# A decoder layer on one core: context values made after the attention, the prologue's loads and steps reordered, the last tile's steps moved

## The reference

```
x = x + attention(layernorm(x))
x = x + cross(layernorm(x), context)
x = x + ffn(layernorm(x))
```

```
K, V = context @ Wh (per head, 2 heads of 128)
A    = max(|sum over batches (Q K^T / sqrt(128) * decay)|, 1)
out  = (relu(x @ wg) * groupnorm(A V)) @ wo
```

## Time and profile before

| what | value |
| --- | --- |
| device time, three runs | 262.43 us median (260.69 to 265.61) |
| profiled execution | 264.52 us |
| its span | 262.4 us |
| PE, DVE, ACT, POOL busy | 239.2, 148.8, 129.0, 92.3 us |
| prologue, to the masks of tile 0 | 0 to 23.7 us |
| tiles 0 to 6 | 23.7 to 102.0 us |
| last tile, to cross_mix | 102.0 to 125.8 us |
| cross attention, router, experts, output | 125.8 to 262.4 us |

### The profile page before, as it was taken

How to read it: one execution, slowest core, us unless ns; L and a number is a source line. 1 busy time by engine, 2 the same in 40 slices (tenths; PEclk the granted TensorE clock), 3 DMA queues, 4 the chain that set the end, 5 groups by cost and what they waited for, 6 DMA issues and landing times.

```text
span 262.4 us, 5169 instructions
## 1 busy us (share of the span) xinstructions
PE 239.2 (91%) x1628; PEld 176.7 (67%) x1628; DVE 148.8 (57%) x451; ACT 129.0 (49%) x465; POOL 92.3 (35%) x109
## 2 busy tenths in 40 slices
PE   8768879899999999968787999989999999999995
PEld 6437356666675677847565878756777777777783
DVE  1456827798788877532789569845233232232275
ACT  1124787898898978830052522503433443333340
POOL 2110201111211111010266101464777777777461
PEclk9959999999999999988999999999999999999999
DMA  7999987500000620000001300032232333334396
GB/s 209 238 344 346 368 202 189 152 5 4 4 0 2 224 91 0 4 0 2 0 0 40 122 0 1 5 100 80 71 111 100 102 100 100 106 102 112 104 317 227
DMA packets 20852, 28.10 MB, mean 107 GB/s; under 512 B 2833, under 2 KB 17819, under 8 KB 20827
## 3 DMA queue, kind: packets, MB, share of 16 engines
q1 hardware_dynamic: 16683, 19.01, 24.1%
q0 software_dynamic: 2976, 8.13, 10.2%
q10 hardware_dynamic: 1167, 0.65, 1.0%
HBM read 21.62 MB, written 6.16 MB: 106 GB/s over the span
## 4 chain that ended last, share of the span: by engine, by line
PE 54%; issue 13%; ACT 11%; DMA 9%; DVE 8%; POOL 2%; SPq 1%; ACTq 1%; POOLq 0%; DVEq 0%
PE bank L882 13%; PE bank L894 8%; ACT pr_s L991 7%; PE bank L813 7%; PE bank L522 5%; DMA lnkv_s<-in_ln_kv 4%; PE bank L863 3%; DMA x_s<-expert_out 2%; PE bank L873 2%; PE bank L527 2%; PE bank L570 2%; PE bank L555 2%; PE bank L645 1%; PE bank L498 1%; ACT prT L981 1%
## 5 line engine op out<-in xcount | busy, mean ns | idle before, releaser
L991 ACT ACTIVATE pr_s<-bank,mx 128x128 f32<-128x128 f32 x128 | 45.3, 383 | 9.6 <-DVE mx L1221 9.0
L882 PE MATMUL bank<-gu_s,bxT 128*128 x124 | 41.7, 460 | 0.2 <-DVE bxT L1544 0.2
L1550 DVE TENSOR_TENSOR pr_s<-bank,pr_s 128x176 f32<-128x176 f32 x31 | 10.6, 341 | 51.7 <-ACT pr_s L1150 50.9
L483 POOL DMA_INDIRECT expert_out<-by,prT x31 | 31.1, 1004 | 15.1 <-ACT by L981 7.7
L478 POOL DMA_INDIRECT qx_s<-ffn_in,prT x31 | 30.1, 972 | 14.5 <-issue 8.2
L981 ACT ACTIVATE prT<-bank 128x512 f32<-128x512 f32 (+1 forms) x63 | 30.7, 497 | 2.2 <-PE bank L570 1.2
L894 PE MATMUL bank<-dn_s,prT 88*128 x124 | 31.7, 379 | 0.0
L991 ACT ACTIVATION_READ_ACCUMULATOR pr_s<-bank,mx 128x1 f32 x128 | 28.6, 223 | 0.0
L882 PEld LDWEIGHTS bank<-gu_s,bxT 128*128 128x128 f32 x124 | 21.2, 190 | 7.2 <-issue 0.4
L570 PE MATMUL bank<-tab,pr_s 128*128 128x128 f32 x128 | 19.5, 275 | 5.4 <-ACT prT L981 2.8
L1221 DVE TENSOR_REDUCE mx<-bank 128x4 f32<-128x512 f32 x32 | 20.4, 682 | 5.9 <-PE bank L555 5.8
(11 more groups left out here) (192 smaller groups left out, 428.8 us busy)
## 6 DMA issues: line engine op xcount, KB each, us to landing
gu_s<-in_w_gu SPq DMA_DIRECT2D x8, 704.0 KB, 8.7
dn_s<-in_w_dn SPq DMA_DIRECT2D x4, 704.0 KB
qx_s<-in_ctx_in SPq DMA_DIRECT2D x2, 512.0 KB, 10.5
ffn_in<-x_s SPq DMA_DIRECT2D x4, 256.0 KB, 2.1
cv_s<-expert_out SPq DMA_DIRECT2D x4, 256.0 KB, 4.3
x_s<-expert_out SPq DMA_DIRECT2D x4, 256.0 KB, 6.0
out<-x_s SPq DMA_DIRECT2D x7, 128.0 KB, 4.0
gu_s<-in_x_t SPq DMA_DIRECT2D x1, 768.0 KB, 12.4
```

Of the source, the lines that this page charges most:

```text
L483: pool.indirect_dma_start(expert_out[:], bass.IndirectOffsetOnAxis(ap=idx[:, 1, k:k + 1], axis=0), by[:, k % RB, :], None).then_inc(dma_sc ...
L882: last = mm(bank[2 + i % 2][:, 0:2 * I], bxT[:, i % 2, k, :], gu_s[:, k, bass.ds(e, 1), :], start=k == 0, stop=k == KD - 1)
L991: last = nc.scalar.activation(pr_s[:, n % 2, h, :], score_bank(n)[:, h * T:(h + 1) * T], ACT.Exp, bias=mx[:, n % 4, h:h + 1], accum_out=de ...
L1550: V.tensor_tensor(bh[:, i % 2, :], bank[2 + i % 2][:, I:2 * I], bs[:, i % 2, :], ALU.mult).then_inc(dve_hidden, 1)
```

## The change

- **Loads.** The layer-norm constants become columns of the table, and identity, rope, head and layer-norm columns come in one DMA on ACT's queue, which then has three DMAs where it had six. x tile 1 moves from sixth to third place on SP's queue. The context is held in the first half of gu_s[:, 1], where it can stay longer; the two expert-weight loads for that half move behind a wait for all context values, ahead of the ffn_in stores on SP's queue.
- **Prologue order.** `qk_transpose(0)` directly follows `keys_values(0)` and stands ahead of `latent_transpose(1)`; on VectorE `q_out(0)` goes ahead of `latent_normalize(1)`; the statistics of x tiles 4 to 7 move into tile 0.
- **Context keys and values.** Both context-key steps of group 1 stay in tile 0 but stand later; all four context-value steps move behind the attention, with their copies.
- **Last tile.** Gates (2,1) move behind `out_project(6)`, the cross scores are spread between the last steps, the denominators of tile 7 are computed ahead of the variance of tile 6, the last denominators' transpose goes to bank 5 and the last probabilities' to bank 0, and `out_project(7)` stands ahead of `cross_transpose(6)`.

The core of the diff:

```diff
-        lnq_s = sb("lnq_s", [128, 2])
-        lnkv_s = sb("lnkv_s", [KPH, 2, 2])
+        lnq_s = tab[:, C_LN:C_LN + 2]
+        lnkv_s = tab[0:KPH, C_LN + 2:C_LN + 6].rearrange("p (k n) -> p k n", k=2)
...
-        cT = qx_s[:].rearrange("p b k t -> p (b k t)")[:, 0:B * D].rearrange("p (h b t) -> p h b t", h=XH, b=B)
+        cT = gu_s[:, 1, 0:E // 2, :].rearrange("p e n -> p (e n)")[:, 0:B * D].rearrange("p (h b t) -> p h b t", h=XH, b=B)
...
             sp.dma_start(x_s[:, 0:1, :], xv[:, 0:1, :]).then_inc(ld_x[0], 16)
+            sp.dma_start(x_s[:, 1:2, :], xv[:, 1:2, :]).then_inc(ld_x[1], 16)
             sp.dma_start(wht_s, wh_t.rearrange("h p n -> p h n")).then_inc(ld_wh_t, 16)
             sp.dma_start(cT[:, :, 0:4, :], ctx_in[:, :, 0:4, :]).then_inc(ld_ctx0, 16)
             sp.dma_start(wkv_s[:], w_kv.rearrange("(k p) n -> p k n", p=KPH)).then_inc(ld_w_kv, 16)
-            sp.dma_start(x_s[:, 1:2, :], xv[:, 1:2, :]).then_inc(ld_x[1], 16)
...
-            for k, e in ((0, 0), (0, 4), (0, 8), (0, 12), (1, 0), (1, 4)):
+            for k, e in ((0, 0), (0, 4), (0, 8), (0, 12)):
                 expert_weights(k, e)
...
+            sp.wait_ge(pe_ctx_values, B // 2)
+            expert_weights(1, 0)
+            expert_weights(1, 4)
...
             def ctx_values(g, j):
                 if g == 0:
                     pe.wait_ge(ld_wh, 16)
-                    pe.wait_ge(act_ctx_keys, j + 1)
+                    pe.wait_ge(act_probs_T, NC * B - 2) if j else pe.wait_ge(act_exp, NC * B - 1)
                 else:
-                    pe.wait_ge(act_keys_values, 3) if j else pe.wait_ge(dve_qk_T, 2)
+                    pe.wait_ge(act_ctx_values, j + 1)
...
             queries(0)
             keys_values(0)
+            qk_transpose(0)
             latent_transpose(1)
-            ctx_values(0, 0)
-            qk_transpose(0)
-            ctx_values(0, 1)
             pe.wait_ge(ld_table_b, 16)
-            pe.wait_ge(act_ctx_values, 2)
+            pe.wait_ge(act_ctx_keys, 2)
             pe.wait_ge(dve_qk_T, 1)
...
-            act.dma_start(tab[:, C_ID:C_ID + 128], table[:, C_ID:C_ID + 128]).then_inc(ld_identity, 16)
-            act.dma_start(tab[:, C_ROPE:C_DECAY], table[:, C_ROPE:C_DECAY]).then_inc(ld_table, 16)
-            act.dma_start(lnq_s[:], ln_q).then_inc(ld_ln, 16)
-            act.dma_start(lnkv_s[:], ln_kv.rearrange("(k p) n -> p k n", p=KPH)).then_inc(ld_ln, 16)
+            act.dma_start(tab[:, 0:C_DECAY], table[:, 0:C_DECAY]).then_inc(ld_table, 16)
             act.dma_start(wq_s[:], w_q).then_inc(ld_w_q, 16)
             wh_square_out()
             ctx_keys_out(0, 0)
-            act.wait_ge(ld_ln, 32)
+            act.wait_ge(ld_table, 16)
...
             latent_variance(1)
+            q_out(0)
             latent_normalize(1)
-            q_out(0)
             qk_out(0)
-            x_variances(2, B)
+            x_variances(2, 4)
...
                 if tiles(i + 2):
                     query_latents_out(i + 2)
+                if i == 0:
+                    x_variances(4, B)
+                if i == B - 1:
+                    denominators(i)
                 if tiles(i - 1):
                     x1_variance(i - 1)
-                if i >= B - 2:
+                if i == B - 2:
                     x1_normalize(i - 1)
-            denominators(B - 1)
             rdT_out(B - 1)
             out_normalize(B - 1)
+            x1_normalize(B - 2)
             residual_attention(B - 1)
```

More of the change, by code:

```diff
@@ L102, in bf16_constants, with decoder_layer @@
     return c.astype(mybir.dt.np(mybir.dt.bfloat16))
-def decoder_layer(nc, x, x_t, ctx_in, table, table_b, table_r, w_m, w_q, w_kv, w_out, ln_q, ln_kv, wh, wh_t, wg, wo, gn,
+def decoder_layer(nc, x, x_t, ctx_in, table, table_b, table_r, w_m, w_q, w_kv, w_out, wh, wh_t, wg, wo, gn,
                   gate, w_gu, w_dn, s_gu_d, s_dn_d, out):
@@ L427, in _ @@
             rsqrt_latent(1)
-            rsqrt_x(3, 2, B)
+            rsqrt_x(3, 2, 4)
             for i in range(B):
@@ L716, in _ @@
                     gates(2, 0)
-                    gates(2, 1)
                 if tiles(i + 1):
@@ L724, in _ @@
                     out_project(i - 1)
-                if i == 0:
-                    ctx_values(1, 0)
+                if i == B - 1:
+                    gates(2, 1)
+                    cross_scores(0)
                 if tiles(i + 2):
                     latent_transpose(i + 2)
+                if i == 0:
+                    ctx_keys(1, 1)
                 prob_transpose(n + 2)
@@ L731, in _ @@
                     cross_transpose(i - 2)
+            cross_scores(1)
             prob_transpose(NC * B - 1)
+            cross_scores(2)
+            weigh_values(NC * B - 4)
+            weigh_values(NC * B - 3)
+            weigh_values(NC * B - 2)
             rden_transpose(B - 1)
-            for c in range(NC):
-                weigh_values(NC * (B - 1) + c)
+            weigh_values(NC * B - 1)
+            cross_scores(3)
+            out_project(B - 1)
             cross_transpose(B - 2)
-            cross_scores(0)
-            cross_scores(1)
-            out_project(B - 1)
-            for b in range(2, B - 1):
-                cross_scores(b)
+            ctx_values(0, 0)
+            cross_scores(4)
+            cross_scores(5)
+            ctx_values(0, 1)
+            cross_scores(6)
             cross_transpose(B - 1)
-            cross_scores(B - 1)
+            ctx_values(1, 0)
+            cross_scores(7)
+            ctx_values(1, 1)
             gates(3, 0)
@@ L1090, in _ @@
             x1T_out(B - 2)
+            ctx_values_out(0, 0)
+            ctx_values_out(0, 1)
             x1T_out(B - 1)
+            ctx_values_out(1, 0)
+            ctx_values_out(1, 1)
             def yT_out(q):
@@ L1606 @@
     a = "L0_attn_"
+    table = constants()
+    table[:, C_LN:C_LN + 2] = _np.stack([g[a + "q_ln_w"], g[a + "q_ln_b"]], 1)
+    table[0:KPH, C_LN + 2:C_LN + 6] = _np.stack([g[a + "kv_ln_w"], g[a + "kv_ln_b"]], 1).reshape(2, KPH, 2).transpose(1, 0, 2).reshape(KPH, 4)
     arrays = {
@@ L1610 @@
         "ctx_in": g["ctx_2048"].reshape(B, T, XH, HD).transpose(3, 2, 0, 1),
-        "table": constants(),
+        "table": table,
         "table_b": bf16_constants(),
```

68 lines of the change are left out of this document (29 added, 39 removed).

## The result

| | kernel before | changed kernel |
|---|---|---|
| median, runs beside each other | 262.41 us (260.69 to 265.61) | 254.82 us (253.69 to 255.44) |
| ratio, 95% interval | | 0.973 [0.966, 0.979] |
| the same in two later comparisons | 263.94, 263.76 | 254.43, 254.55: 0.967 [0.961, 0.974] and 0.964 [0.957, 0.971] |
| profiled execution, its span | 264.52, 262.4 | 254.44, 252.4 |

A forecast was written before the change was run, and what follows sets the result against it. Bounds: a wait chain entered by the kv layer-norm constants' load, ScalarE's in-order context work in tiles 0 and 1, TensorE at the attention's end. -2.0 - 3.7 - 1.4 = -7.1 from the 262.43 median gives 255.3 us; range 251.5 to 259.5.

The forecast's parts named there:

- Start of the queries: Prologue: without the wait for the layer-norm constants' load, the query projection starts at 14.4 for 15.47 us, a gain of 1.1.
- Tiny packets that each take a turn: Prologue: the 1.3 KB constants' load is late because packets under 512 B, 40 of 127, take turns between large ones.
- The 0.5 charged for the second x tile ahead of Wh: Prologue: 128 KB of x ahead of the transposed Wh delays the path by 0.4 to 0.6 us, taken as 0.5.
- Rival B: Prologue: w_kv, landing at 15.4, sets the queries' start, so the 1.1 us gain is lost: 256.4 us; chance 0.15.
- Queries to masks(0): Prologue: qk transposes directly after ScalarE's copies, then VectorE's copies, make this stretch 7.3 for 8.26 us, a gain of 0.96.
- rival D: Prologue: with less idle the clock stays up, queries and keys/values run at 2.4 GHz, -2.1 us more: 253.2; chance 0.08.
- the idle ahead of the latent transposes and a short one before the queries remain: Prologue: the argument against the clock staying up, which would have given -2.1 us more.
- Tiles 0 and 1: First attention tiles: context work leaving ScalarE's chain gains 2.4 us in tile 0 and 1.3 in tile 1, together -3.7.
- Rival C: First tiles: TensorE's and VectorE's pipeline filling, not ScalarE, holds masks(1); gain 1.2 and not 3.7: 257.8 us; chance 0.15.
- E: Context values had filled waits early, nothing is won in the prologue, the end pays 4.4 us: 266.8, slower; chance 0.04.
- The end: Attention's end: four value steps add 3.8 us to TensorE, the upper clock returns 1.7; cross mix 124.4 for 125.78, -1.4.
- Later stages: Cross mix to the end, 136.6 us: nothing edited, no change; a change above 0.5 us would make the forecast wrong.

## Why the prediction was right, and where it was not

**Start of the queries (-1.1; -1.4 to -1.9 in the changed kernel's three profiles against the first of before, -0.6 to -1.1 against the second).** The chain's row pointed at the right load and the forecast at the wrong reason. "Tiny packets that each take a turn" was not it: the same tiny loads cost nothing once w_kv is behind them or spread. Nor did the merging do it in this kernel; either edit keeps the constants off w_kv's queue, merging fully, the new order mostly. The 0.5 charged for the second x tile ahead of Wh was near (Wh landed at 6.1 and 6.2 before, 6.5 to 6.9 in the changed kernel) and became the term that sets the start. Rival B (w_kv, 15.4) fell: w_kv landed at 12.9 to 14.0 and is the last wait in one profile of three, by 0.07.

**Queries to masks(0) (-0.96; -3.27).** The mechanism was right and its size, 1.2 to 1.4, a little above the 0.96: hand-overs took less than the 0.5 assumed. From the end of ScalarE's value copy to masks(0) it is 2.04, and 1.7 of that are transposes and VectorE's copies. The rest, 1.9 to 2.1, is the clock: rival D, held at 0.08 and priced at 2.1, is what happened, and its price was right. The step that failed is "the idle ahead of the latent transposes and a short one before the queries remain": they did (1.35 and 0.53), and the clock stayed up all the same. Masks(0) moved by -5.1 in all, outside the -0.9 to -2.9 given for the prologue.

**Tiles 0 and 1 (-3.7; -4.2).** Right in sum and inside its bounds, -3.2 and -1.0 for -2.4 and -1.3. It was worked out along ScalarE's queue, and the copies are worth 0.4 of it. Of the 0.8 by which tile 0 beat the forecast, half is VectorE: its qk copies were kept at their old place, 33.2 or 9.5 behind masks(0), and ended 9.05 behind them; masks(1) followed 0.84 later and not 1.2. The steady 10.63, taken as a floor for tile 1 (10.96), is none for tile 0, which ran in 9.89; it has no earlier tile to weigh and project. Rival C (1.2 of gain) and E (masks(1) still 13 behind) fell with the 9.89.

**The end (-1.4; -2.44, at the edge of its bounds).** -0.8 from order and -1.65 from the clock. The forecast had the clock's return at 1.7, and the work behind at 3.8 for 3.0 measured (a step is 0.9, and cost less where it filled the pipeline); what it underestimated is how much could be hidden, since it did not see that the old order had 3.9 us of waits and the new one without values still 1.9. Of 3.0 us of values only 1.1 lengthened the stretch. Its statement that TensorE is the bound there holds to 0.04 us. The residual moved as said: 14.88 behind masks(7) for 18.33, 3.5 earlier for "about 3".

**Later stages (0; +1.94).** "I am wrong if any later stage changes by more than 0.5" was met. Cross mix to the shared experts is +1.13, all of it the lower clock level from 121 to 124.2: the same stretch is 18.76 in the second and third profile for 18.83 before. From there to the last expert block it is the same to 0.1 us. The rest, up to 1.5, is in the last 10 us: VectorE's last shared product stands in order behind the sums of gathered expert outputs, and those wait for gathers of 4 to 6 us whose end varies. Over the changed kernel's three profiles it lies 132.9 to 133.9 behind the cross mix (the clock's 1.13 taken off), before 132.3. From the cross mix to the end of the span all nine profiles of the changed kernel and of those made from it take 136.6 to 138.2 (1.2 taken off where the clock dropped in between), before 136.6 in its one profile outside the slower chip; so the change does not always cost something here, and whether it does on average is open. The moved expert weights cost nothing that a trace shows.

**The sum (-7.1).** Order alone, by the stretches at the upper level and the estimate for the prologue: start -1.4 and -0.6 (from 15.47 and 14.74 to 14.11), queries to masks(0) -1.4 and -1.3, tiles 0 and 1 -4.2, the five tiles -0.15, the end -0.8. Together -7.9 and -7.1, beside -7.0 to -7.9 from the executions with the clock up. The forecast had 5.4 of order and 1.7 of clock. Tiles gave 0.7 and the end 1.1 more order than forecast, and the prologue between 0.1 less and 0.7 more. So the sum was the price of the order by luck: the 1.7 put down to the clock stood in for order that was priced too low. And what the clock gave on top in the profiled pair, at the front above all, was about what the profiled execution of before lay above its median, 2.1; taking the sum off the median and not off the profiled time is what kept it out. The recorded bounds "251.5 to 258.5" do not follow from the three parts: those add to -9.7 and -2.7, which from the median is 252.7 to 259.7. The 254.82 lies in either.

## What to carry to other kernels

Before a late small load is merged or moved, look at which load's landings it follows: loads of the same awkward row count can queue behind each other however small they are (85 rows here), and giving the large one a partition count that spreads it cured both. Work that waits on another engine's bank costs its wait and whatever stands in order behind its consumer, more than its own time: put it where the engine has waits anyway, and price it there by the waits (3.0 us of matmuls cost 1.1 here). One part's price depends on what else is late: the reordering of the prologue is worth 0.6 with the second x tile early and 1.4 together with moving it. And part the clock from the order before a profiled pair is read term by term, with one more profile of each kernel or the two edits crossed.

## What the runs showed of the hardware

- Two loads of 85 rows had five late landing events each, in pairs 0.2 to 0.3 us apart, as if on the same five DMA engines; a 1.3 KB load landed 0.2 us behind the 319 KB one ahead of it. In 96 partitions 360 KB landed at 9.9 where 319 KB in 85 had landed at 13.2.
- A stretch of 3.4 us at the lower clock level cost 1.0 (an estimate, prologue) to 1.7 us, 6.8 us cost 2.9 at the end of the attention (25.0 for 22.13) and 1.9 to 2.1 in the prologue, where part of the way waits for a load and not for TensorE.
- Two chips differ by 11 us for the same kernel (medians 264 and 275), and the profiles put it all behind the cross mix (149.4 us of span for 136.6); the attention's tiles take 10.63 us on both.
